# Softmax denominators in four groups of 32 array columns, in an attention and feed-forward kernel on eight cores

## What is computed

```python
n = layernorm(x)
q, k, v = n @ Wq + bq, n @ Wk + bk, n @ Wv + bv      # 16 heads of 64
q, k = rope(q), rope(k)
scores = q @ k.T / sqrt(64), causal mask
attn = softmax(scores, axis=-1)
x = x + (attn @ v) @ Wo + bo
n = layernorm(x)
h = silu(fp4(n) @ fp4(w_gate).T) * (fp4(n) @ fp4(w_up).T)
x = x + fp4(h) @ fp4(w_down).T
```

## Time and profile before

| | |
|---|---|
| time, median of 3 runs | 1258.13 us (1257.23 to 1261.32) |
| the profiled execution: its own time | 1265.16 us |
| span of its slowest core (core 7) | 1263.4 us |
| spans of the eight cores | 1245.5 to 1263.4 us |
| granted TensorE clock, mean of core 7 | 0.959 |
| busy in the span of core 7: PE, DVE, ACT | 1082.6, 1040.8, 765.0 us |

### The profile page before, as it was taken

The page is one execution under the profiler, slowest core; times in us unless marked ns, Lnnn a source line. Parts: engine busy times, 40 slices in busy tenths (PEclk is TensorE's granted clock), DMA queues, the critical chain, the costliest instruction groups (busy, mean ns, idle before and its releaser), DMA issues.

```text
span 1263.4 us, 18188 instructions; the slowest of 8 cores (1245.5 to 1263.4 us)
## 1 busy us (share of the span) xinstructions
PE 1082.6 (86%) x6112; PEld 454.2 (36%) x6112; DVE 1040.8 (82%) x1199; ACT 765.0 (61%) x1000; POOL 104.1 (8%) x203
## 2 busy tenths in 40 slices
PE   0798898988898887877898699999998988999996
PEld 0343232333233222322233254444444444444443
DVE  4598998688888969898875688888888888888885
ACT  3577888878788976888655544443443444344432
POOL 1011011111111110112310000000000000000000
PEclk9899999999999997998999899999998999999998
DMA  9968677678878694779999200000000000000000
GB/s 206 253 112 168 138 159 160 123 152 163 167 145 173 138 139 112 149 172 249 207 250 335 80 1 34 34 34 34 35 35 34 34 24 27 17 34 34 17 18 33
DMA packets 108923, 139.94 MB, mean 111 GB/s; under 512 B 76256, under 2 KB 79776, under 8 KB 107936
## 3 DMA queue, kind: packets, MB, share of 16 engines
q1 hardware_dynamic: 91792, 90.27, 31.2%
q0 software_dynamic: 15312, 42.22, 16.1%
q10 hardware_dynamic: 1728, 6.29, 1.5%
HBM read 96.29 MB, written 27.13 MB: 98 GB/s over the span
## 4 chain that ended last, share of the span: by engine, by line
DVE 36%; PE 26%; ACT 13%; issue 13%; DMA 11%; DVEq 1%; POOL 1%; SPq 0%; ACTq 0%; POOLq 0%
PE ps L683 7%; PE ps L971 5%; DVE sm_bm L300 5%; DVE h_u L1342 4%; PE ps L927 4%; ACT PT L953 4%; DVE h_u L314 4%; DVE h_u L327 3%; DVE h_y L332 3%; PE ps L654 3%; PE ps L1311 3%; ACT h_y L319 3%; DVE sm_bm L309 2%; DMA qx<-wd 2%; DVE hqb L337 2%
## 5 line engine op out<-in xcount | busy, mean ns | idle before, releaser
L953 ACT ACTIVATE PT<-ps,nb 128x1024 bf16<-128x1024 f32 (+1 forms) x320 | 301.4, 992 | 13.6 <-PE ps L927 6.7
L1355 PE MATMUL ps<-wdT,hqT 128*128 128x512 bf16 x704 | 179.7, 413 | 42.6 <-DVE x_t L1372 37.1
L319 ACT ACTIVATE h_y<-h_u 128x1024 f32<-128x1024 f32 (+1 forms) x48 | 47.3, 985 | 239.9 <-DVE h_u L314 239.9
L1311 PE MATMUL ps<-wgT,xqT 128*128 128x512 bf16 (+1 forms) x768 | 170.4, 365 | 6.0 <-ACT h_u L1333 4.4
L1311 PE MATMUL ps<-wuT,xqT 128*128 128x512 bf16 (+1 forms) x768 | 168.6, 363 | 0.0
L927 PE MATMUL ps<-qk 64*128 64x512 bf16 (+3 forms) x640 | 117.7, 360 | 50.1 <-ACT PT L953 31.2
L683 PE MATMUL ps<-xlT,wqk 128*128 128x512 bf16 x512 | 125.3, 389 | 27.1 <-ACT PT L953 25.9
L971 PE MATMUL ps<-PT,vat 128*64 128x512 bf16 (+3 forms) x640 | 122.3, 379 | 0.4
L1355 PEld LDWEIGHTS ps<-wdT,hqT 128*128 128x128 bf16 x704 | 72.6, 105 | 138.9 <-issue 71.9
L971 PE MATMUL ps<-PT,ones 128*64 128x512 bf16 (+3 forms) x640 | 114.8, 356 | 0.0
L327 DVE SCALAR_TENSOR_TENSOR qx<-qy,qx 128x1024 f32<-128x1024 f32 (+1 forms) x68 | 80.6, 1186 | 29.0 <-ACT qy L319 29.0
(11 more groups left out here) (94 smaller groups left out, 1485.4 us busy)
## 6 DMA issues: line engine op xcount, KB each, us to landing
qx<-wu SPq DMA_DIRECT2D x22, 512.0 KB, 5.7
qx<-wg SPq DMA_DIRECT2D x22, 512.0 KB, 5.5
x_a<-x SPq DMA_DIRECT2D x16, 512.0 KB, 17.1
qx<-wd SPq DMA_DIRECT2D x16, 512.0 KB, 5.2
x_t<-x POOLq DMA_DIRECT2D x16, 512.0 KB, 7.2
out<-x_t SPq DMA_DIRECT2D x16, 512.0 KB, 2.6
sw<-qk POOLq DMA_DIRECT2D x56, 128.0 KB, 5.3
rb<-rscr POOLq DMA_DIRECT2D x28, 256.0 KB, 6.2
```

The costliest lines, as they stand in the source:

```text
L319: return act((lambda c: c.activation(y[:, 0:F], u[:, 0:F], AFT.Abs, scale=2.0 ** 22)), [(sDVE, v4)] + list(y_free))
L953: exp_a[n] = act((lambda c: c.activation(PT[j].ap()[:, :, o:512], sc[:, :, o:512], AFT.Exp, bias=nb12.ap(), scale=0.125)), ws, cost=0.31 + ...
L1311: ins = te.matmul(bank[:, 0:cn], xqT[t % 2].ap()[:, kc, :], w.ap()[:, n0:n1, kc, :], start=(kc == 0), stop=(kc == KC - 1))
L1355: ins = te.matmul(psO[:, nh * 512:(nh + 1) * 512], hqT[q % 2].ap()[:, jj, :], wdT.ap()[:, 4 * nh:4 * nh + 4, j, :], start=(j == 0), stop=( ...
```

## The change

`av` no longer computes the denominators with 64 columns of ones for each head in every step. It takes 32 columns for each head, and in the blocks 1 to 3 it leaves them out in even steps and makes up for them in the odd ones: four matmuls side by side, two for the even step's tile (array columns 0 to 63) and two for the odd one's (64 to 127), each group adding up its own part. In block 0 the two matmuls of the first half are done in every step, and at its first step a matmul with a matrix of zeros clears the other half. The gather fetches both parts (four DMAs in place of two), an addition on VectorE joins them, and the reciprocal follows on it. The tile of an even step is released with the odd one's. The planner's costs of `av` and of the reciprocal change with it. `dn` moves to another place in SBUF.

```diff
-    ones64 = misc("ones64", [128, 64], BF16, 128)
+    ones32 = misc("ones32", [128, 32], BF16, 64)
+    zero64 = misc("zero64", [128, 64], BF16, 128)
...
-    dn = [misc(f"dn{i}", [128, 32], F32, 128) for i in range(2)]
+    dn = [at(f"dn{i}", OFF_E + 2560 + 256 * i, [128, 2, 32], F32)
+          for i in range(2)]
...
-            v.memset(ones64[:], 1.0)
+            v.memset(ones32[:], 1.0)
+            v.memset(zero64[:], 0.0)
...
             for h in range(2):
-                d = dma("gpsimd", sDN[k],
-                        dn[k].ap()[64 * h:64 * h + 64, 0:w],
-                        den.ap()[64 * h:64 * h + 1, a:b]
-                        .rearrange("o (p f) -> o p f", f=w), ws)
+                for e in range(2):
+                    r = 64 * e + 32 * h
+                    d = dma("gpsimd", sDN[k],
+                            dn[k].ap()[64 * h:64 * h + 64, e, 0:w],
+                            den.ap()[r:r + 1, a:b]
+                            .rearrange("o (p f) -> o p f", f=w), ws)
...
+            v1 = dve((lambda v: v.tensor_tensor(
+                rn[k].ap()[:, 0:w], dn[k].ap()[:, 0, 0:w],
+                dn[k].ap()[:, 1, 0:w], Alu.add)), ws, cost=0.2)
             nrm["recip"][i] = dve((lambda v: v.reciprocal(
-                rn[k].ap()[:, 0:w], dn[k].ap()[:, 0:w])), ws, cost=0.5)
+                rn[k].ap()[:, 0:w], rn[k].ap()[:, 0:w])), [(sDVE, v1)],
+                cost=0.35)
...
+            side = qb > 0
+            last = kc == 4 * qb + 3
+
+            def ones(te, e, c, m):
+                ins = None
+                oo = width(qb, c)
+                for h in range(2):
+                    r = 64 * e + 32 * h
+                    ins = te.matmul(
+                        od[r:r + 32, 512 + oo:1024], ones32[:],
+                        PT[m % NPT].ap()[:, h, oo:512],
+                        start=(c == e), stop=last or (side and c == 4 * qb + 2),
+                        skip_group_check=True)
+                return ins
+
             def f(te):
                 ins = None
-                for dst, w in ((0, None), (512, ones64)):
-                    for h in range(2):
-                        lhs = (vat.ap()[:, p + 1, kc, 64 * h:64 * h + 64]
-                               if w is None else ones64[:])
+                for h in range(2):
+                    ins = te.matmul(
+                        od[64 * h:64 * h + 64, o:512],
+                        vat.ap()[:, p + 1, kc, 64 * h:64 * h + 64],
+                        PT[j].ap()[:, h, o:512], start=(kc == 0),
+                        stop=last, skip_group_check=True)
+                if not side:
+                    ins = ones(te, 0, kc, n)
+                    if kc == 0:
                         ins = te.matmul(
-                            od[64 * h:64 * h + 64, dst + o:dst + 512], lhs,
-                            PT[j].ap()[:, h, o:512], start=(kc == 0),
-                            stop=(kc == 4 * qb + 3), skip_group_check=True)
+                            od[64:128, 512:1024], zero64[:],
+                            PT[j].ap()[:, 0, :], start=True, stop=True,
+                            skip_group_check=True)
+                elif kc % 2:
+                    ones(te, 0, kc - 1, n - 1)
+                    ins = ones(te, 1, kc, n)
                 return ins
...
-                            cost=0.2 + 0.45 * (512 - o) / 512)
+                            cost=0.1 + (0.35 + 0.1 * (kc % 2))
+                            * (512 - o) / 512)
+            if side and kc % 2:
+                pt_free[n - 1] = pt_free[n]
```

## The result

The changed kernel takes 1282.19 us in the median of 4 runs (1275.53 to 1289.49), the kernel before 1259.72 beside it (4 runs, 1257.23 to 1262.21): a ratio of 1.016, 95% interval 1.0117 to 1.0203. It is slower by 20 us or so, where 1259 was predicted and 1267 was the end of the range. In some executions the cores of one die are granted a lower clock and take some per cent longer; all ratios and means here leave those out, and since the profiled executions of e2 and e12 were such ones, their stages are means of the four cores of the other die alone.

A forecast was written before the change was run, and what follows sets the result against it. ScalarE's exponentials pace full-width attention steps, PE the diagonals and block 0. PE -1.0, gather +1.05, additions +0.2 and +0.5 make +0.8 us on 1258.13: 1259 us, range 1251 to 1267.

The forecast's parts named there:

- the planner's: Ordering by costs: little change expected, since `w_max` holds chunks to their step; waits may shift a few us either way.
- The second rival: Last head pair and after: all four gathers' issues or one more chunk behind attention, 4 to 7 us more, 1265; chance 0.25.
- TensorE's: Attention matmuls: 0.60 us gained on diagonals less 0.47 lost in block 0 per head pair, some 1.0 us gained over eight.
- Four side by side: Odd steps of blocks 1 to 3: the four 32-column ones matmuls run together, costing 0.24 us as one pass.
- the change of form: PE switching between matmul shapes, also between 64 and 32 columns: 0.08 us each time.
- block 0's first `av`: First step of block 0, with ones of 32 and zeros added: +0.39 us, near 0.95 us in the timeline after.
- full steps: Full-width steps away from the diagonal: ScalarE sets the pace, so they stay 1.0 us apart.
- PE's waits of the scores for the exponentials: Attention: PE's waits for the exponentials would grow well above 31 us, the gain going into waiting.
- The diagonals' gain: Diagonal steps of blocks 1 to 3: 0.25, 0.25 and 0.10 us gained, 0.60 per head pair.
- block 0's loss: Block 0, per head pair: added form changes and a pass of zeros, 0.47 us lost.
- The gather and the addition: Denominator chain: 1.05 us for the last gather, 0.2 for the last addition and 0.5 for the ten others.
- PE gains more: Attention, rival: no change of form between 64 and 32 columns or more PE-bound steps, 1254.5 to 1252; chance 0.24.

The follow-up runs named there:

- e2: Kernel before with the changed kernel's planner costs and later tile release, old instructions kept; 10.6 us more than before by the mean of its cores.
- e12: e7 with the constant row of ones written in six pieces, five more VectorE writes at the start; worth under 1 us, ratio didn't fall.
- e10: Changed kernel with the load of stored gate tiles issued later and one x load moved back on GpSimd's queue; 6 to 7.5 us better than the changed kernel.
- e6: Changed matmuls with the order and gather of before, fetching only the first part of the denominators; 3.7 us more than before, error 2.0.
- e1: Changed kernel with the planner costs of before, so all new instructions in the old order; ratio 1.008 of before.
- e3: Kernel before, its matmuls and order kept, with ones of 0.5, four gather DMAs and an addition; 1.5 us more than before, error 1.9.
- e13: Kernel before with ones matmuls only for each block's first and last key tile in blocks 1 to 3; 3.2 us slower by the mean of cores.
- e7: e1 with block 0's denominators made by 64-column matrices, half ones and half zeros; 3.5 us more than before by the mean of cores.
- e15: Kernel before with two added matmuls with zeros in the last head pair's 21 full-width steps; that pair became 0.5 to 1 us longer.
- e16: e10 with block 0 as in e7; block 0 took 7.01 us per pair, the feed-forward part is 2 us longer.

## Why the prediction was wrong

**The step that failed** is the planner's: "`w_max` holds the chunks to the step, which is why I expect little", with waits that "come and go, to either side, by a few us". The order cost 8.5 us by e2 and, for what the two loads hold of it, 6 to 7.5 by e10, all to one side. The chunks did stay where they were: three begin behind the last pair in every kernel. What moved was smaller. The planner, told that `av` is shorter, puts the last pair's rotary embedding ahead of the last steps of weight chunks on VectorE; the last store is then issued after a large load on another queue, and a load that waits for that store stands at the head of SyncE's queue. I priced shifts of work between engines, but not the place of a waiting DMA relative to a large one. The second rival looked at the same stretch with the wrong mechanism: its test, a chunk more behind attention, came out negative, while its 4 to 7 us were exceeded.

**The term that was mis-sized** is TensorE's, -1.0 us in the sum. The changed matmuls by themselves cost 3.7 us with an error of 2.0 (e6); the distances of the steps account for 1 to 2 of them. So the new instructions would have missed the 1259 in the old order as well: e1 is 8.6 us over before, some 6 without the pause of the last section, where the sum has 0.8.

**TensorE's terms were right in kind.** Four side by side, as taken; the change of form 0.10 (taken 0.08); block 0's first `av` 0.99 us (0.95); full steps still 1.0 us apart; PE's waits of the scores for the exponentials up to 23.3 us from 18.5 in the seven pairs (the 38.8 us to 615 us, where the earlier trace rows have 31.2, contain one wait of 10.5 that is the hole's), ScalarE's for the projections 40.1 from 42.7. The diagonals' gain was 0.43 us and not 0.60, and block 0's loss 0.58 to 0.72 and not 0.47, so the sum's -1.0 should have been +1 to +2. (Two of its additions are loose, with no effect: 0.16 and 0.24 make 0.40 and not 0.39, and the diagonal's terms 0.27 and not 0.28.)

**The gather and the addition** were 1.75 us in the sum and 1.5 in e3, with an error of 1.9. That fits, but so would nothing.

**PE gains more**, the faster rival at 0.24, is refuted by the result, and e13 shows that there was nothing to gain: with most of the ones gone altogether the kernel is no faster. My reason was only that ScalarE paces the full steps. There is a second, which I didn't have: where work was taken from TensorE in those steps its clock fell, and in e13 block 0 takes 0.8 to 0.9 us longer per pair at it. That this is also why e6 and e7 cost 3.5 us, where the step sums say about none, is argued from their clock (0.952) and the slow projections (8%), not shown; e15 didn't support the converse.

**What stays open**: the 4 us by which e10's last pair is longer than e1's, some 2 us of e6's 3.7, and why block 0 takes 7.01 us in e16 and 6.55 in e7.

## What to carry to other kernels

When a change alters costs that an ordering program reads, the order is a change of its own: run the old instructions in the new order and the new instructions in the old one before any pricing of single operations. In a new order look first at each load that waits for a store, and at what large transfer is issued between the two. And a saving on an engine that isn't the pace-setter can be worth less than nothing: on TensorE it was followed here by a lower granted clock (0.934 from 0.962 in e13) where that engine was the bound.

## What the hardware showed unexpectedly

In the kernel before, VectorE pauses for about 0.35 us once in every two tiles of the feed-forward part, which is every 64 of its busy instructions, between two instructions of its own. Core 3, before and e1, the pause each time in the second and the first row:

```profile
939.80 0.95 DVE L327 SCALAR_TENSOR_TENSOR h_u<-h_y,h_u 128x768 f32<-128x768 f32 x1
941.21 0.96 DVE L332 SCALAR_TENSOR_TENSOR h_y<-h_y,h_u 128x768 f32<-128x768 f32 x1 [0.46 <-DVE h_u L327]
```

```profile
939.77 0.96 DVE L316 TENSOR_TENSOR h_u<-h_u,sm_bm 128x768 f32<-128x768 f32 x1 [0.46 <-DVE sm_bm L311]
```

The first pair of instructions starts 1.41 us apart; the same pair without the pause, in e1, 1.05. In the kernel before it falls where a later wait for ScalarE absorbs it, and each tile takes 34.53 us; in e1 it doesn't, and tiles take 34.88 and 34.53 in turn, in e16 34.89 and 34.54, in e2 34.89 and 34.54. That is the 2.0 to 2.6 us by which their feed-forward part is longer, with no edit in it. What the engine does in the pause no row says. It stands at other instructions where instructions were added far ahead of it (e1), but also in e2, which adds none.
